# Cross-attention over 1444 keys: the array's jobs and the weighings of two key tiles put into one gap

## What is computed

```
q, k, v = heads(x @ Wq.T + bq), heads(ctx @ Wk.T + bk), heads(ctx @ Wv.T + bv)
scores  = q @ k.T / sqrt(8), masked
out     = softmax(scores) @ v        # 1600 rows (16 heads x 100 tokens) by 1444 keys, for each of 32 sequences
```

## Time and profile before

| | before |
|---|---|
| median of three runs | 2277.2 us (2276.39 to 2281.86) |
| span of the profiled execution, first to last instruction | 2267.4 us |
| stage of the change within the span | about 604 to 1731 us |
| TensorE busy, whole span | 1969.0 us (87%) |
| VectorE busy, whole span | 1578.2 us (70%) |
| ScalarE busy, whole span | 1324.7 us (58%) |

### The profile page before, as it was taken

One profiled execution on the slowest core, in us unless ns is written; L12 is line 12 of the kernel. 1 busy time (PEld: TensorE's weight loads), 2 busy tenths in 40 slices (PEclk: granted clock), 3 DMA queues, 4 the chain that ended last, 5 costly groups with the idle time before them and its releaser, 6 DMA issues. The chain is left out here.

```text
span 2267.4 us, 43146 instructions
## 1 busy us (share of the span) xinstructions
PE 1969.0 (87%) x16922; PEld 1258.0 (55%) x16922; DVE 1578.2 (70%) x3726; ACT 1324.7 (58%) x2169; POOL 551.4 (24%) x477
## 2 busy tenths in 40 slices
PE   3679999667999999999999999999997888888997
PEld 2546666444556556565565655556564555555554
DVE  4845666795787877878788788878771566664554
ACT  3645776683366666666666666666664555553444
POOL 1411322314122212222221222222222132311122
PEclk9879999777799999999999999999998788788999
DMA  5025554012132323233131322313222001103441
GB/s 153 1 92 183 184 173 142 4 37 91 65 109 74 126 68 118 78 105 119 68 126 63 120 85 101 121 66 122 79 89 67 16 8 16 31 1 59 67 71 40
DMA packets 120023, 189.26 MB, mean 83 GB/s; under 512 B 36770, under 2 KB 94090, under 8 KB 118414
## 3 DMA queue, kind: packets, MB, share of 16 engines
q1 hardware_dynamic: 119822, 186.50, 26.6%
HBM read 103.33 MB, written 11.76 MB: 51 GB/s over the span
## 5 line engine op out<-in xcount | busy, mean ns | idle before, releaser
L1610 DVE TENSOR_REDUCE b_part_max<-psum 128x1 f32<-128x482 f32 (+3 forms) x1248 | 737.6, 651 | 188.1 <-PE psum L1487 174.1
L1400 ACT ACTIVATE b_PT<-psum 128x800 f32<-128x800 f32 x768 | 616.6, 836 | 386.1 <-PE psum L1506 381.1
L1487 PE MATMUL psum<-b_KH,b_QBD 64*128 64x482 f32 (+1 forms) x1152 | 422.6, 445 | 45.7 <-DVE b_part_max L1610 43.3
L1506 PE MATMUL psum<-b_QS,b_KS 64*128 64x200 f32 x3072 | 438.3, 288 | 0.5 <-ACT b_PT L1400 0.3
L1506 PEld LDWEIGHTS psum<-b_QS,b_KS 64*128 64x128 f32 x3072 | 339.4, 186 | 16.2 <-issue 11.8
L1522 PE MATMUL psum<-b_PT,b_V 128*32 128x200 f32 x6144 | 341.4, 339 | 0.6 <-ACT b_PT L1400 0.6
L1487 PEld LDWEIGHTS psum<-b_KH,b_QBD 64*128 64x128 f32 x1152 | 197.3, 189 | 198.6 <-DVE b_part_max L1610 118.4
L1322 POOL TENSOR_TENSOR b_KL<-b_KF,b_KH 128x1444 fp32r<-128x1444 f32 x32 | 106.8, 3338 | 693.3 <-PE psum L1506 670.1
L1522 PEld LDWEIGHTS psum<-b_PT,b_V 128*32 128x32 f32 x6144 | 159.9, 109 | 149.1 <-ACT b_PT L1400 82.3
L1900 ACT ACTIVATE c_HE<-psum,C 128x400 f32<-128x400 f32 x128 | 75.7, 595 | 94.6 <-PE psum L2116 90.1
L1474 PE MATMUL psum<-W,b_CT 128*128 128x128 f32 (+1 forms) x768 | 117.7, 293 | 12.6 <-DVE b_part_max L1610 6.7
(11 more groups left out here) (280 smaller groups left out, 3095.2 us busy)
## 6 DMA issues: line engine op xcount, KB each, us to landing
b_KS<-b_KH SPq DMA_DIRECT2D x64, 722.0 KB
a_CT<-in_ctxt SPq DMA_DIRECT2D x32, 722.0 KB, 5.5
b_CT<-in_ctxt SPq DMA_DIRECT2D x32, 722.0 KB, 4.4
b_KS<-b_KL SPq DMA_DIRECT2D x32, 722.0 KB
a_CN<-in_ctxn SPq DMA_DIRECT2D x32, 704.0 KB
att_scratch<-b_AO SPq DMA_DIRECT2D x32, 200.0 KB, 1.9
c_G<-gates_scratch SPq DMA_DIRECT2D x4, 1600.0 KB
c_KBD<-gates_scratch SPq DMA_DIRECT2D x4, 1600.0 KB
```

Source lines behind the costliest of these rows:

```text
L1400: nc.scalar.activation(PT[:, kt % 2, 2 * a:2 * a + 2, :], psum[:, 2 * a:2 * a + 2, 0:TG], ACT.Exp).then_inc(sem["pt_ready"], 1)
L1487: m = mm(bank(b, D, size), QBD[rows, j % 2, tile * D:(tile + 1) * D], KH[rows, j % 2, at_:at_ + size], start=True, stop=True)
L1506: m = mm(bank(p, D, 2 * T, (s % 2) * 2 * T), KS[rows, j % 2, s, kt * D:(kt + 1) * D], QS[rows, j % 2, s * 2 * T:(s + 1) * 2 * T], start=Tr ...
L1610: v.tensor_reduce(part_max[0:rows, q, c:c + 1], bank(b, rows, CHUNKS[c][1]), AX.X, ALU.max)\
```

## The change

Every second gap between scores gets no job and no weighing. The order for a pair of loop steps (kt even, kt odd) becomes: scores of tile kt + 1 with `max` jobs, scores of tile kt + 2 with `max` jobs, all jobs of p 4, the weighings of both tiles of the pair. For that the jobs of p 4 move to odd `kt` (`result` stays at 1, values from 2, 3, 4 to 1, 3, 5, left maxima from 5, 6, 7 to 3, 5, 7, keys from 6, 7, 8 to 7, 9, 9, `turn` from 8 to 9, queries from 0 and 5 to 1 and 9), `MAIN_TILES` puts four `max` jobs at kt 1 and 6 and none at 7, `PT` gets a third buffer, and ACT copies values and keys one step after the new places.

```diff
-MAIN_TILES = ((9, 2, 2), (10, 2, 2), (11, 2, 2), (0, 2, 2), (1, 2, 1), (2, 1, 2), (3, 2, 1), (4, 1, 2), (5, 2, 1), (6, 1, 2), (7, 1, 1))
-QUERY_SLOTS = (((0, 0), (1, 0), (2, 0), (3, 5)), ((4, 0), (5, 5)), ((6, 0),), ())
+MAIN_TILES = ((9, 2, 2), (10, 2, 2), (11, 2, 2), (0, 2, 2), (1, 2, 2), (2, 1, 2), (3, 2, 1), (4, 1, 2), (5, 2, 1), (6, 2, 2))
+QUERY_SLOTS = (((0, 1), (1, 1), (2, 1), (3, 9)), ((4, 1), (5, 9)), ((6, 1),), ())
+VALUE_SLOTS, LEFT_SLOTS, KEY_SLOTS = (1, 3, 5), (3, 5, 7), (7, 9, 9)
+RESULT_SLOT, TURN_SLOT = 1, 9
...
-    jobs = [((g, j + 1, "result", 0), PHASES * 1 + 4)]
+    jobs = [((g, j + 1, "result", 0), PHASES * RESULT_SLOT + 4)]
...
-        jobs += [((g, j + 1, "value", r), PHASES * (r + 2) + 4) for r in range(3)]
-        jobs += [((g, j + 1, "max", len(MAINS) + c), PHASES * (c + 5) + 4) for c in range(3)]
-        jobs.append(((g, j + 1, "turn", 0), PHASES * 8 + 4))
+        jobs += [((g, j + 1, "value", r), PHASES * VALUE_SLOTS[r] + 4) for r in range(3)]
+        jobs += [((g, j + 1, "max", len(MAINS) + c), PHASES * LEFT_SLOTS[c] + 4) for c in range(3)]
+        jobs.append(((g, j + 1, "turn", 0), PHASES * TURN_SLOT + 4))
...
-        jobs += [((g, j + 2, "key", r), PHASES * (r + 6) + 4) for r in range(3)]
+        jobs += [((g, j + 2, "key", r), PHASES * KEY_SLOTS[r] + 4) for r in range(3)]
...
-        PT = sb("PT", [D, 2, HG, TG])
+        PT = sb("PT", [D, 3, HG, TG])
...
-                    wait(act, sem["pv_done"], n * KT + (kt - 1))
-                nc.scalar.activation(PT[:, kt % 2, 2 * a:2 * a + 2, :], psum[:, 2 * a:2 * a + 2, 0:TG],
+                    wait(act, sem["pv_done"], n * KT + (kt - 2))
+                nc.scalar.activation(PT[:, kt % 3, 2 * a:2 * a + 2, :], psum[:, 2 * a:2 * a + 2, 0:TG],
...
-                        if kt - 3 in range(len(highs)):
-                            value(*place(g, j, highs[kt - 3]), g, j + 1, kt - 3)
-                        if kt - 8 in range(len(keys)):
-                            high_keys(*place(g, j, keys[kt - 8]), g, j + 2, kt - 8)
+                        for i, at in enumerate(highs):
+                            if kt == VALUE_SLOTS[i] + 1:
+                                value(*place(g, j, at), g, j + 1, i)
+                        for i, at in enumerate(keys):
+                            if kt == KEY_SLOTS[i] + 1:
+                                high_keys(*place(g, j, at), g, j + 2, i)
...
-                               PT[:, kt % 2, 2 * b + r // 2, (r % 2) * 2 * T:(r % 2 + 1) * 2 * T],
+                               PT[:, kt % 3, 2 * b + r // 2, (r % 2) * 2 * T:(r % 2 + 1) * 2 * T],
...
-                        weigh(g, j, kt)
+                        if kt % 2:
+                            weigh(g, j, kt - 1)
+                            weigh(g, j, kt)
```

## The result

The changed kernel takes 2437.7 us (four runs, 2435.8 to 2446.2) against 2279.5 us: ratio 1.071, interval 1.068 to 1.074. The forecast of 2389 us has the right sign and about 70% of the loss (112 of 158 us); the measured time lies 6 us above the range. The span grew from 2267.4 to 2434.0, and all of it is in the changed stage: from the first to the last `result` job 1126.8 us before, 1293.3 after (601.6 to 1894.9). The spans differ by 167 us and the medians by 158, because a run's time lies only 1.8 us above its span here (2435.83 against 2434.0): the profiled execution before the change was about 8 us shorter than the median of 2277.2, so most of the 9.8 us that the prediction carries over does not lie around the span.

The account below looks back on a forecast made before the run. PE looked like the bound, with its matmuls waiting on DVE's bank ring and ACT's exponentials. 31 items x (4.08 - 0.62) = 107, plus 4 for the last, together +111.5 on 2277.2: 2389 us, range 2335 to 2432.

Parts of the forecast that it names:

- The chains: Waits of paired scores for exponentials and DVE-drained banks: pairs sum to 38.18 against 34.10 us, +4.08 an item.
- D: Tile pair kt 6 and 7: scores end at 3.30 us; with left, key and two weighings 6.21 us.
- E: Tile pair kt 8 and 9: first key waits until 3.50 us; with two keys and two weighings 7.06 us.
- two weighings: Both weighings of a tile pair in a row at its end: 1.54 us, bounds 1.64 to about 1.34.
- ring wait: At kt 8 and 9, the first key waits for the third maximum's bank, done at about 3.50 us.
- Queries: Query jobs in the paired order: 1.36 us an item instead of 2.00, -0.62 after rounding.
- rival 3: PE's clock falls, adding 15 us an item in a fifth of the items: 93 us, 2482 us; chance 0.04.
- Rival 1: Exponentials alone bind, DVE catches up during two weighings: 2.84 us an item lost, 2301 us; chance 0.08.
- Rival 2: PE's changes of shape cost far more than seen and the waits are filled: faster, 2223 us; chance 0.06.
- Rival 4: The waits added are just paid for by what the change saves: about 2277 us; chance 0.03.
- Parts costed at nothing: Third PT buffer and ACT's copies one step later: no cost, the copies covered by two weighings.
- F: Tile pair kt 10 and 11, eight maxima and no job: scores 3.92 us, with two weighings 5.46 us.

Follow-up runs that it names:

- second dose of fill: Changed kernel with repeated maximum matmuls: first ahead of second scores three times (not kt 6), second and third twice at kt 10, 11, 0, 1: 2393.6 us, 1.049.
- The fills: Maximum matmuls repeated in PE's waits: in the changed kernel (second dose of fill) 1.049; with maxima spread three per tile over kt 0 to 7, 2352.6 us, 1.034.
- first dose: Changed kernel with the first maximum's matmul ahead of every second scores, and the last maximum's at kt 6, issued three times: 2446.3 us, 1.072.

## Why the prediction fell short

**The chains held, and were somewhat over-sized.** The second dose of fill, which keeps the chains, shows four undisturbed items in a row (its `result` jobs):

```profile
765.90 0.94 PE L1474 MATMUL psum<-b_OD,K 128*128 128x200 f32 x4
...
806.00 0.94 PE L1474 MATMUL psum<-b_OD,K 128*128 128x200 f32 x4
...
845.12 0.94 PE L1474 MATMUL psum<-b_OD,K 128*128 128x200 f32 x4
...
883.68 0.94 PE L1474 MATMUL psum<-b_OD,K 128*128 128x200 f32 x4
...
920.97 0.94 PE L1474 MATMUL psum<-b_OD,K 128*128 128x200 f32 x4
```

They take 40.10, 39.12, 38.56 and 37.29, together 155.07 against the 144.39 of the earlier trace rows: 2.67 us an item. With 31 items and 4 us for the last that is 87 us, where the forecast had 111.5. Its scores were right to 0.05 in every pair; its gaps were too dear: `result` and value 1.77 instead of 1.95, left and key in D 1.17 instead of 1.37, turn and two keys in E 2.27 instead of 2.55, two weighings 1.50 instead of 1.54. Jobs that stand together overlap more than their distances in the old order show, and E's ring wait was shorter: its first key starts at 3.43, where the prediction wrote about 3.50 (its own terms, 1.82 + 0.52 + 0.66 + 0.57, give 3.57). Together 0.9 an item. Queries cost 1.48 an item instead of the 1.36 of the forecast (2.00 before).

**The step that failed is the clock.** The sum keeps PE at 1.00 throughout and so puts the clock at nothing; its fall is only rival 3, with a chance of 0.04. In the changed kernel it fell in nearly every item, on top of the chains: 167 less 87 leaves about 80 us. The fills show 49 of them directly. The rest is read from the `result` jobs of the two kernels, the first and the 31st, before the change and then after it:

```profile
604.49 0.94 PE L1469 MATMUL psum<-b_OD,K 128*128 128x200 f32 x4
...
1681.62 0.94 PE L1469 MATMUL psum<-b_OD,K 128*128 128x200 f32 x4
```

```profile
601.61 1.70 PE L1473 MATMUL psum<-b_OD,K 128*128 128x200 f32 x4
...
1824.77 0.94 PE L1473 MATMUL psum<-b_OD,K 128*128 128x200 f32 x4
```

These 30 items take 1077.1 us before and 1223.2 after; at the undisturbed lengths above they would take 7 x 155.07 + 2 x 37.29 = 1160.1. So 83 us of their growth are chains and 63 come with the falls. The last two items grow by 20.5 more, some 14 of it beyond their chains.

The argument against the fall was that the last item has such waits and keeps 1.00. That compared the wrong thing: the earlier trace rows has matmuls in flight for 16.49 of 16.70 us there, so its waits hardly leave PE empty. The old last item waits for the same exponentials but has a weighing inside each wait and needs 3.78 for a pair; the new one would need 4.50 at full clock, by the forecast, with the same matmuls. The 0.30 of the earlier trace rows, cited as the wait itself, was also taken in a stretch whose clock is 0.50 (596 to 603 us).

Two errors of opposite sign met: chains over-sized by 24 us and the clock left out with some 80. That the time lies only 6 us above the range is in part luck. So is the price of rival 3 (93 us, a fifth of the items), which is nearly right for the wrong places: nearly every item has one or two short falls, and the last one long one. The upper end of the range adds up to 2435, not 2432; the measured time lies above both. Two 40.4 us stretches of the middle, about an item each, and the last, in the changed kernel (PE alone; busy time, granted clock, DMA share, GB/s):

```profile
1126.80:1167.20 40.40, 37.51 (x369) 0.96 0.25 86
1167.20:1207.60 40.40, 37.06 (x358) 0.92 0.25 86
...
1854.00:1894.40 40.40, 35.18 (x319) 0.58 0.10 25
```

A row of 0.96 is 3.2 us at 1.2 GHz, one of 0.92 is 6.5; all but two of the 32 such rows lie between 0.91 and 0.96.

**Rival 1** (exponentials alone) is out: with half the maxima, the pairs with eight lose 0.84. **Rival 2** (dear changes of shape) is out: with both waits cut and the clock at 1.00 the new order is 38 us behind. The Trainium skill's rule (TensorEngine Tiling (Array Packing), Key Properties: a change of tiling mode drains the array) agrees in kind: two weighings in a row take 1.50, two apart 2 x 0.82 = 1.64, so a removed round gives back 0.14 us there, a fifth of the 0.68 from which it would have decided. **Rival 4** is out by the time itself.

**Parts costed at nothing** held: the third buffer and the moved copies, with the moved jobs, cost 0.3% in all when the weighings stand apart. The turn's four transfers are issued from 1813.03 to 1815.23, and the next item's first scores start at 1817.31, 2.01 after the pair's first scores instead of 1.80. What the 0.2 are was not tried; F's length of 3.91 shows that nothing hangs on them.

## What to carry to other kernels

A gap that looks like a loss (a change of the array's shape, 0.14 us) may be the cover of a longer wait (0.8 us for an exponential that frees the bank): before moving work out of a gap, ask what the engine will stand and wait for in its place, and work the chain out from the rows. When such waits put together thin PE's work, look at the granted clock too, and treat its fall as an addition to the sum, not as an alternative. Whether a matmul can be added for nothing depends on its place: in waits it gave 2% in two kernels here, on the chain it took as much, and the first dose, with a part of it on D's chain, gave nothing.

## What the runs showed of the hardware

The clock fell with PE never idle for long: in the scores of that pair D (its busy row is above), two waits of 0.30 and 0.33 us and 3.07 us in flight out of 3.70, and then 0.50. PE's longest wait in the whole stage is 1.0 us. In TensorE: Matmul & The Clock Gate the Trainium skill (HAM oscillation) tells of a kernel whose clock falls because PE waits for transfers between bursts of matmuls; no wait of that kind stands before the falls here, only several short ones for ACT and DVE. Redundant matmuls inside those waits brought the clock's mean over the stage from 0.95 to 0.99 and from 0.93 to 0.98. They add work and shorten the waits at once, so these runs do not tell which of the two counts. With half the maxima the scores of a pair with eight took 3.07 instead of 3.91, and the mean rose to 0.98 without an added matmul. What the chip asks for was not looked for.
